# A fused attention and mixture-of-experts layer: the end of its feature loop rearranged, and the softmax sums given semaphores of their own

## The reference

```python
q, k, v = split(x @ Wq), split(x @ Wk), split(x @ Wv)
amp(t)  = softplus(t) / sqrt(mean(softplus(t)**2) + 1e-6)      # per head
phi     = pi * tanh(x @ Wqp), pi * tanh(x @ Wkp)
q_cos, q_sin = amp(q) * cos(q_phi), amp(q) * sin(q_phi)        # k alike
scores  = (q.k + lam_h * (q_cos.k_cos + q_sin.k_sin)) / 4      # causal
x1      = layernorm(x + softmax(scores) @ v @ Wo)
out     = layernorm(x1 + moe(x1))      # 8 experts, top 2, silu(h1*h3)
```

## Time and profile before

| | |
|---|---|
| median of three runs | 1925.81 us (1922.15 to 1928.32) |
| the profiled execution, its own time | 1924.49 us |
| its span from first to last instruction | 1922.8 us |
| mean granted TensorE clock | 0.946 of full |
| PE busy | 1736.4 us, 90% of the span |
| DVE, ACT, POOL busy | 1244.2, 898.1, 332.6 us |
| feature loop / attention / the rest, about | 0 to 250 / 250 to 1276 / 1276 to 1923 us |

### The profile page before, as it was taken

How to read it: one execution, slowest core, us unless ns; L and a number is a source line. 1 busy time by engine, 2 the same in 40 slices (tenths; PEclk the granted TensorE clock), 3 DMA queues, 4 the chain that set the end, 5 groups by cost and what they waited for, 6 DMA issues and landing times.

```text
span 1922.8 us, 28296 instructions
## 1 busy us (share of the span) xinstructions
PE 1736.4 (90%) x9130; PEld 910.4 (47%) x9131; DVE 1244.2 (65%) x2992; ACT 898.1 (47%) x1043; POOL 332.6 (17%) x468
## 2 busy tenths in 40 slices
PE   6999779999999999999999999977639999999965
PEld 3544334444444444444444444336516666666644
DVE  3688777777777777777777777326435555555536
ACT  2876754555555555555555554644402222222236
POOL 0000011021111211211112112114561111111111
PEclk9999889999999999899999999987659999999988
DMA  3464436020020110200201103036421111111144
GB/s 105 156 238 174 166 128 224 2 98 15 29 78 7 64 44 7 100 13 25 82 8 65 47 2 128 7 107 218 169 77 43 49 44 44 44 47 47 44 134 153
DMA packets 99595, 155.32 MB, mean 81 GB/s; under 512 B 10880, under 2 KB 60832, under 8 KB 99104
## 3 DMA queue, kind: packets, MB, share of 16 engines
q1 hardware_dynamic: 85088, 122.57, 19.4%
q0 software_dynamic: 14400, 31.37, 4.6%
HBM read 87.90 MB, written 65.35 MB: 80 GB/s over the span
## 4 chain that ended last, share of the span: by engine, by line
PE 69%; issue 7%; ACT 5%; DVE 4%; DMA 2%; SPq 1%; POOL 1%; ACTq 0%; POOLq 0%; DVEq 0%
PE att_ps_s L1017 23%; PE exp_ps_h L1649 13%; PE att_ps_o L1036 12%; PE att_ps_m L266 10%; PE exp_ps_y L1667 6%; ACT att_probs L1064 3%; PE exp_ps_t L1657 2%; DMA out_parts<-att_out_t 1%; PE exp_ps_x L1638 1%; DVE att_maxima L276 1%; POOL att_probs L1119 1%; DVE fin_stats L1180 1%; DVE fin_res L1870 0%; DVE fin_mixed L1863 0%; PE fin_ps_y L1221 0%
## 5 line engine op out<-in xcount | busy, mean ns | idle before, releaser
L1064 ACT ACTIVATE att_probs<-att_ps_s 128x1024 f32<-128x1024 f32 (+3 forms) x640 | 563.0, 895 | 461.8 <-PE att_ps_s L1017 454.3
L1017 PE MATMUL att_ps_s<-att_queries,att_keys 49*128 49x512 f32 (+3 forms) x2560 | 626.4, 557 | 17.8 <-ACT att_probs L1064 12.2
L276 DVE TENSOR_REDUCE att_maxima<-att_ps_m 128x1 f32<-128x512 f32 x768 | 487.4, 684 | 152.1 <-PE att_ps_m L266 147.5
L266 PE MATMUL att_ps_m<-att_keys,att_queries 48*128 48x512 f32 (+3 forms) x1280 | 493.6, 591 | 20.4 <-DVE att_maxima L279 14.7
L266 PEld LDWEIGHTS att_ps_m<-att_keys,att_queries 48*128 48x128 f32 x1280 | 190.5, 187 | 323.6 <-DVE att_maxima L276 149.9
L1017 PEld LDWEIGHTS att_ps_s<-att_queries,att_keys 49*128 49x128 f32 x2560 | 241.1, 189 | 125.1 <-ACT att_probs L1064 87.9
L279 DVE CUSTOM_DVE_ANT_0 att_ps_m<-att_ps_m,att_future 128x128 f32<-128x128 f32 (+3 forms) x512 | 240.5, 514 | 69.6 <-PE att_ps_m L266 68.3
L1036 PE MATMUL att_ps_o<-att_probs,att_values 128*32 128x512 f32 (+3 forms) x2560 | 273.3, 543 | 12.1 <-POOL att_probs L1119 12.1
L1649 PE MATMUL exp_ps_h<-keep_w,exp_rows_t 128*128 x568 | 261.8, 604 | 5.2 <-DVE exp_rows_t L1683 5.2
L1725 ACT ACTIVATE exp_hidden<-exp_product 128x512 f32<-128x512 f32 x71 | 44.9, 632 | 347.5 <-DVE exp_product L1708 347.5
L1119 POOL TENSOR_SCALAR_AFFINE_SELECT att_probs<-att_probs 128x512 f32<-128x512 f32 x128 | 81.1, 634 | 480.2 <-ACT att_probs L1064 480.1
(11 more groups left out here) (179 smaller groups left out, 1426.3 us busy)
## 6 DMA issues: line engine op xcount, KB each, us to landing
att_queries<-q_parts SPq DMA_DIRECT2D x64, 192.0 KB
att_keys<-k_parts SPq DMA_DIRECT2D x64, 192.0 KB
exp_rows<-sorted_rows SPq DMA_DIRECT2D x71, 129.0 KB, 2.3
v_rows<-pre_v_sb SPq DMA_DIRECT2D x8, 1024.0 KB, 4.8
q_parts<-pre_waves SPq DMA_DIRECT2D x16, 512.0 KB, 5.7
k_parts<-pre_waves SPq DMA_DIRECT2D x16, 512.0 KB, 6.3
att_values<-v_rows SPq DMA_DIRECT2D x32, 256.0 KB
out_parts<-att_out_t POOLq DMA_DIRECT2D x32, 256.0 KB, 6.1
```

Source lines behind the costliest of these rows:

```text
L266: pe.matmul(bank[:, 0:width], self.queries[g % 2][half, c, r, P * q:P * q + P], self.keys[g % 2][half, k, r, 0:width], start=True, stop=Tr ...
L276: dve.tensor_reduce(to, bank[:, 0:width], AX.X, ALU.max).then_inc(self.s_mr, 1)
L1017: mm = pe.matmul(score_tile(unit, first, last)[:, e], keys[g % 2][half, k // TPC, r, P * (k % TPC):P * (k % TPC) + P].bitcast(F32), querie ...
L1064: act.activation(probs[:, step % PROBS, DUO * r:DUO * r + DUO, first:last], score_tile(unit, first, last), ACT.Exp, scale=SCALE).then_inc( ...
```

## The change

In the feature loop:
- ACT: the two waves of chunk 6 move behind everything else of iteration 9, right ahead of those of chunk 7. The last table loads are then those of exp (chunk 6's norm), ln, exp, sine, and attention's exp.
- DVE: the amplitude of chunk 7 moves one iteration forward, ahead of chunk 5's last product; the absolute phase of chunk 7 moves ahead of four of chunk 6's products.
- PE and DVE: eight more pairs of maxima (40 early in place of 32), three ahead of chunk 7's norm matmuls and of chunk 6's normed amplitude, five behind them. The turned rows keep their place, ahead of these; the first two extra tiles therefore wait for the copies of the rows (`s_row`).

In attention: the sums' DMA has its own semaphore `s_sums`, and the inverse waits only for that. The inverse is planned 4.5 us behind the copy in place of 6, and POOL's store of it is an event of its own, 0.8 us behind that. The planner takes ACT to be free at 9 us (before 8) and DVE at 15 us (before 8).

```diff
-SWITCH, SEEN, PLACED, SETTLED, EAGER, TAIL = 200, 200, 2200, 6000, 300, 8000
+SWITCH, SEEN, PLACED, SETTLED, KEPT, EAGER, TAIL, DVE_TAIL = 200, 200, 2200, 4500, 800, 300, 9000, 15000
...
-EARLY_GROUPS = len(EARLY_CHUNKS) * EARLY_TURNS
+LOOP_TILES = DUO * len(EARLY_CHUNKS) * EARLY_TURNS
+MORE, FIRST_MORE = 8, 3
+EARLY_GROUPS = len(EARLY_CHUNKS) * EARLY_TURNS + MORE
...
-            if tile >= len(self.ring):
+            if tile in range(LOOP_TILES, LOOP_TILES + len(self.ring)):
+                pe.wait_ge(self.s_row, tile - LOOP_TILES + 1)
+            elif tile >= len(self.ring):
                 pe.wait_ge(self.s_mr, tile - len(self.ring) + 1)
...
                 (project_v, 1),
+                (lambda i, p: send_more(FIRST_MORE) if i == NCH - 1 else None, 2),
                 (lambda i, p: sum_norm(i, p, Q), 2),
                 (turn, 0),
                 (lambda i, p: sum_norm(i, p, K), 2),
+                (lambda i, p: send_more(MORE - FIRST_MORE) if i == NCH - 1 else None, 2),
...
                 (lambda i, p: norm_exp(i, p) if i == NCH - 1 else None, 2),
-                (make_waves, 2)])
+                (lambda i, p: make_waves(i, p) if i == NCH - 2 else None, 3),
+                (lambda i, p: make_waves(i, p) if i != NCH - 2 else None, 2)])
...
-                (amplitudes, 2),
+                (lambda i, p: amplitudes(i, p) if i < NCH - 1 else None, 2),
+                (lambda i, p: take_more(FIRST_MORE) if i == NCH - 1 else None, 2),
...
                 (norm_amplitudes, 3),
+                (lambda i, p: abs_phase(i, p) if i == NCH - 1 else None, 2),
+                (lambda i, p: take_more(MORE - FIRST_MORE) if i == NCH - 1 else None, 2),
...
-                (abs_phase, 2),
+                (lambda i, p: abs_phase(i, p) if i < NCH - 1 else None, 2),
                 (take_early, 1),
                 (lambda i, p: query_features(i, p, 1), 3),
                 (keep_v, 1),
+                (lambda i, p: amplitudes(i, p) if i == NCH - 1 else None, 1),
                 (lambda i, p: key_features(i, p, 1), 3),
...
-        self.free = dict(pe=0, dve=TAIL, act=TAIL, pool=0)
+        self.free = dict(pe=0, dve=DVE_TAIL, act=TAIL, pool=0)
...
         n = self.settling.pop(0)[1]
         self.run("dve", 260, 0)
         self.events.append(("invert", n))
+        self.keeping.append((self.free["dve"] + KEPT, n))
+
+    def keep_inverse(self):
+        self.events.append(("keep_inverse", self.keeping.pop(0)[1]))
...
                     if n >= 2:
-                        dve.wait_ge(s_store[n % 2], 32 * (n // 2))
+                        dve.wait_ge(s_store[n % 2], 16 * (n // 2))
+                        dve.wait_ge(s_sums[n % 2], 16 * (n // 2))
                     dve.tensor_copy(out_t[:, n % 2], ps_o[:, :]).then_inc(s_oc, 1)
 
             def invert(n):
-                dve.wait_ge(s_store[n % 2], 32 * (n // 2 + 1))
+                dve.wait_ge(s_sums[n % 2], 16 * (n // 2 + 1))
...
-                    pool.dma_start(sums[:, n % 2], out_t[HD:P:VW, n % 2]).then_inc(s_store[n % 2], 16)
+                    pool.dma_start(sums[:, n % 2], out_t[HD:P:VW, n % 2]).then_inc(s_sums[n % 2], 16)
...
-                elif event == "invert":
+                elif event == "keep_inverse":
                     store_inverse(*what)
```

More of the change, by code:

```diff
@@ L309, in turn_early @@
     def turn_early(self, pe, ident):
-        pe.wait_ge(self.s_mr, DUO * EARLY_GROUPS)
+        pe.wait_ge(self.s_mr, LOOP_TILES)
         for n in range(EARLY_ROWS):
@@ L529, in sum_norm, with send_more @@
                 mm.then_inc(s_norm, 1)
+            def send_more(count):
+                for _ in range(count):
+                    maxima.send_early(pe)
             pipelined(pe, NCH, [
@@ L690, in take_early, with take_more @@
                     maxima.take_early(dve)
+            def take_more(count):
+                for _ in range(count):
+                    maxima.take_early(dve)
             def turn_early(i, p):
@@ L741, in __init__ @@
         self.unit = self.value = self.group = 0
-        self.slots, self.turns, self.settling = [], [], []
+        self.slots, self.turns, self.settling, self.keeping = [], [], [], []
         self.exp_at, self.masked_at, self.summed_at = [], {}, []
@@ L854, in made @@
                 self.invert()
+                continue
+            if self.keeping and self.keeping[0][0] <= now:
+                self.keep_inverse()
                 continue
@@ L876, in made @@
             self.invert()
+        while self.keeping:
+            self.keep_inverse()
         return self.events
@@ L883, in ring_slots @@
     counts = {"max": DUO * EARLY_GROUPS, "turn_max": EARLY_ROWS}
-    taken, slots = [("turn_max", n + 1) for n in range(EARLY_ROWS)] + [(None, 0)], []
+    taken, slots = [("max", counts["max"] - 1), ("max", counts["max"]), (None, 0)], []
     for kind, *_ in plan:
@@ L923, in attend @@
     last_event = max(i for i, event in enumerate(plan) if event[0] == "values")
-    late = [event[1] for event in plan[last_event:] if event[0] == "invert"]
-    plan = [event for i, event in enumerate(plan) if i <= last_event or event[0] != "invert"]
+    late, late_kept = ([event[1] for event in plan[last_event:] if event[0] == kind] for kind in ("invert", "keep_inverse"))
+    plan = plan[:last_event + 1]
     with ExitStack() as stack:
@@ L951, in attend @@
         s_bias = n_.sem("expert_biases_loaded")
+        s_sums = [n_.sem(f"sums_moved{i}") for i in range(2)]
         s_inv = n_.sem("inverse_ready")
@@ L1143, in _ @@
                     store(*what)
-                elif event == "invert":
+                elif event == "keep_inverse":
                     store_inverse(*what)
         def store_last_inverses(pool):
-            for n in late:
+            for n in late_kept:
                 g, c = divmod(n, QC)
@@ L1346, in _ @@
                 last_quad = ((i // QC + 1) * NQ - 1) * QC + i % QC
-                sp.wait_ge(attended.s_store[last_quad % 2], 32 * (last_quad // 2 + 1))
+                sp.wait_ge(attended.s_store[last_quad % 2], 16 * (last_quad // 2 + 1))
                 sp.wait_ge(attended.s_kept[last_quad % 2], 16 * (last_quad // 2 + 1))
@@ L1537, in _ @@
             for i in range(2):
-                pool.wait_ge(attended.s_store[i], 32 * CHUNKS // 2)
+                pool.wait_ge(attended.s_store[i], 16 * CHUNKS // 2)
                 pool.wait_ge(attended.s_kept[i], 16 * CHUNKS // 2)
```

## The result

The changed kernel took 1897.43 us (median of 4 runs, 1897.17 to 1903.75); the kernel before, on the same chip, 1923.98 us (4 runs, 1919.14 to 1928.32). The ratio is 0.9869, with a 95% interval of 0.9843 to 0.9894: 26.6 us less by the medians. The forecast was 1894, the range 1886 to 1912. The profiled execution of the changed kernel was the slowest of its four: 1903.75 us, span 1902.1 (before: 1924.5 and 1922.8), so its rows show 20.7 us of the 26.6.

The account below looks back on a forecast made before the run. PE, busy for 90% of the span, was taken as the bound, so PE's idle time counted. Savings of 8.0 + 10.0 + 1.5 + 10.7 + 1.3 = 31.5 us from 1924.5 gave 1893.0, by the median 1894; range 1886 to 1912.

Parts of the forecast that it names:

- The loop end, 8.0: End of feature loop: earlier ACT chain and eight early pairs save 8.0 us at the first quad's last chunk.
- The stalls between quads, 10.0: Attention, between quads: an earlier inverse waiting only for the sums removes 10.0 of PE's 10.8 us behind POOL masks.
- DVE's waits, 1.5: Attention: DVE's 13.7 us of waits for the output DMA go, saving PE 1.5 us of waits for maxima.
- My cover of 1.6 us: Between quads: POOL's fourth mask, free at 522.5, beats the end of PE's previous matmuls, 524.06, by 1.6 us.
- The clock, 10.7: Attention: without the longer stalls, three falls of PE's granted clock go, saving 10.7 us (4.0, 4.0 and 2.7).
- The line that I drew: Between quads: clock falls follow stalls of 1.43 us and more, none follows 0.72 to 1.42; under 1 us is safe.
- Route, 1.3: Route, after attention: DVE's residual no longer waits behind the inverse for the last output DMA and starts 1.3 us earlier.
- At nothing: Attention: the added event and the extra wait before the output copy cost nothing.
- Rival 1: Between quads: PE's clock falls all the same, adding 10.7 us to the forecast, 1905 us; chance 0.2.
- Rival 2: Feature-loop end: PE cold at norm matmuls, DVE ends at 255, so 8 us becomes 1: 1901 us; chance 0.17.
- Rival 3: Quad ends: sums' semaphore comes no earlier than the output's, stalls and falls stay, gain 9.3 us: 1916 us; chance 0.1.
- Rival 4: Between quads: the inverse's earlier store holds up POOL's masks if sums land over 7 us after issue: 1945 us; chance 0.03.

Follow-up runs that it names:

- e5: Changed kernel with the inverse planned 6 us behind the copy again instead of 4.5, all else as changed: 1887.61 us.
- e2: Changed kernel with the attention part undone (shared semaphore, inverse at 6 us, store in the same event), new feature-loop end kept: 1914.56 us.
- e7: Changed kernel with SP's two 2 MB loads of expert weights put behind the landing of the first quad's last row of maxima: 1893.85 us.
- e1: Kernel before with nothing but the sums' own semaphores, plan and every engine's order unchanged: 1900.43 us.
- e4: Changed kernel with SP's loads of the next but one quad waiting until the sums of the quad's last chunk have landed: 1887.66 us.
- e6: Changed kernel with the inverse at 6 us and SP's quad loads held behind the sums of the last chunk: 1886.71 us.
- e10: Changed kernel with reciprocal at 6 us, quad loads behind the sums, and expert weights behind the first quad's last row of maxima: 1883.28 us.
- e11: Changed kernel with reciprocal and store of the inverse back in one event 6 us behind the copy; loop end and own semaphores kept: 1890.76 us.

## Why the prediction held, and where it did not

*The number.* 1894 was forecast and 1897.4 measured (1900.8 in the second set). It is near for a mixed reason, and in part by luck. Its terms for the stalls, DVE's waits and the clock, 22.2 us, were sized as they would be only for a kernel whose reciprocal comes behind the sums (e5), and the changed kernel is not that one: its window got 11.1. And of these, 4.6 were busy time saved by the new order, which I had not foreseen; my own terms gave 6.6. The medians, moreover, differ by 26.6 us where the profiled execution, the slowest of the four, shows 20.7.

*The loop end, 8.0:* 7.6 in the profile, 7.9 in e2 alone. The steps were right: five table loads, DVE's maxima 9.5 us earlier (9.7 by my sum), first exp 1.9 us earlier (between my 3.2 and nothing). Not seen: the row's DMAs now meet SP's weights in flight, 5.0 us in place of 1.9, and PE waits 1.7 us more (3.38 against 1.65); e7 shows it. I had put the saving at DVE's end and not asked which transfer would be beside the row at the new time. My 8.0 was a rounding between 6.5 and 9.7, and so took this in by chance.

*The stalls between quads, 10.0, and DVE's waits, 1.5:* this step failed. Measured, PE's idle time in the window fell by 3.2 us, not 11.5. The failing sentence is "though the sums that it needs had landed at 515.4 + 2.9 = 518.3". They had not; the 2.9 came from a semaphore with two DMAs on it. With the 6.6 us of e1 they land near 522. A reciprocal at 520.1 to 521.2 waits then at every quad's end, which I foresaw only for the last. My cover of 1.6 us also left out the mask's own 0.6. e5, which comes later, does not wait and gets the whole. The row that said otherwise was the earlier trace rows, 6.6 us for the same DMA; I took the exception for the exception. The Trainium skill (DMA: Bandwidth & Descriptors, Why a DMA increments its semaphore by 16 and not by 1) warns of two DMAs in flight on one semaphore: its count may pass before the first has landed. That is about waits; the rows of before and e1 show that a reader of landing times is misled by the same thing.

*The clock, 10.7:* 3.4 us by the granted clock, of the 8.0 us by which PE's busy time fell. It failed with the term before it: the stalls had moved, not gone. Three falls are left in the window, at stalls of 0.80, 1.38 and 2.52 us. In e5, with those stalls gone, no fall was left, and busy time was 14.4 us lower than before. The mechanism held, more firmly than three falls could show. In the windows B of all fourteen profiled executions there are 22 falls, and each begins in a stall of PE of 0.8 us or more or within 2.3 us of its end; the six whose stalls there stay under 0.5 us (e1, e4, e5, e6, e10, e11) have none. The line that I drew between stalls below and above 1.43 us did not hold: 0.80 us to 764.4 was followed by a fall at 766.7, 2.14 us to 893.6 by none.

*Route, 1.3:* nothing. The sums alone, 7.5 us from issue to landing there, kept the reciprocal until 8.5 us behind the copy.

*At nothing:* the extra wait ahead of the output's copy shows no wait, as said.

*The rivals.* Rival 1 (the clock falls anyway) is out: in e1 and e10 it does not fall between 339 and 1240 us. Rival 2 (the start gives nothing) is out by A. Rival 3 had the right fact, over 6 us to landing in every quad, and the wrong consequence: the time by it would be 1916, and e1 with 6.3 to 7.2 us to landing had 1900.4, since their semaphore still comes 1.9 us ahead of the output's, enough for a reciprocal 8.2 us behind the copy. (Its 9.3 us also counted the 1.3 of Route, which its own condition rules out.) Rival 4's condition, over 7 us, was met at three quads' ends of the changed kernel (7.1, 7.7 and 8.1), without its result: POOL's store now stands behind the masks, so the wait went to DVE and reached PE through the maxima, up to 2.5 us each, not 3.2 through POOL.

*What is open.* The median of the changed kernel varied by 3.3 us between its two sets of runs, and its clock fell for 20.5 us in one profile's window and for 10.2 in the other's, with nearly the same total of stalls. Why one stall brings a fall and the next does not, and what in the new order saves 4.6 us of busy time, no run here tells.

## What to carry to other kernels

A landing time read from a semaphore that several DMAs share is no landing time of any one of them; look for a place where the same DMA stands alone, or give it its own semaphore, before moving a wait to it. A wait that moves ahead of its data on an in-order engine is paid by whatever is queued behind it: 1.5 us in the planner's constant was worth 10 us or more here, and the best place was the late one. Where an engine's work ends earlier, ask which transfer will be in flight at the new time: small DMAs on the critical path want the big loads issued behind them.

## What the runs showed of the hardware

A DMA of 8 KB between parts of SBUF took 2.3 to 2.6 us to landing at the quads' ends with SP's loads of rows held back (e4), and 6.3 to 8.1 us with them in flight (e1, e5 and the changed kernel); one of 4 KB took 1.6 us without and 5.0 us with SP's loads of 2 MB in flight (e7 and the changed kernel). A stall of PE can cost more in granted clock than it lasts, but not each time: of the changed kernel's seven at the quads' ends, 0.65 to 2.52 us long, three had a fall of 3.4 to 10.2 us, 1.7 to 5.1 us lost at half speed, which began 0 to 2.3 us behind the stall. e1 and e10, without those stalls, had no fall between 339 and 1240 us.
